# Cross attention on one Trainium2 core: the second token tile's queries are copied before the spread reciprocals instead of behind the first exponentials

## The reference, cut to what matters

```python
def _L0_xattn_ref(q, k, v, Wc, bc):          # q: layernorm of x; k = v = ctx_512
    b, s, _ = q.shape
    qh = q.reshape(b, s, N_GROUPS, HEADS_PER_GROUP, HEAD_DIM).transpose(0, 2, 3, 1, 4)
    kh = k.reshape(b, s, N_GROUPS, HEAD_DIM).transpose(0, 2, 1, 3)
    vh = v.reshape(b, s, N_GROUPS, HEAD_DIM).transpose(0, 2, 1, 3)
    scores = jnp.einsum('bghsd,bgtd->bghst', qh, kh) * scale
    probs = jax.nn.softmax(scores, axis=-1)
    out = jnp.einsum('bghst,bgtd->bghsd', probs, vh)
    out = out.transpose(0, 3, 1, 2, 4).reshape(b, s, D_MODEL)
    return out @ Wc.T + bc
x = x + _L0_attn_ref(_layernorm(x), ...)
x = x + _L0_xattn_ref(_layernorm(x), ctx_512, ctx_512, L0_xattn_Wc, L0_xattn_bc)
x = x + _L0_ffn_ref(_layernorm(x), ...)
```

## Time and profile before

| | |
|---|---|
| median of 3 runs | 2202.17 us |
| the profiled execution's own time | 2202.18 us |
| its span, first to last instruction | 2200.5 us |
| TensorE busy | 2022.2 us, 92% |
| VectorE busy | 1703.6 us, 77% |
| ScalarE busy | 1501.7 us, 68% |
| GpSimd busy | 702.2 us, 32% |
| mean granted TensorE clock | 0.962 |

### The profile page before, as it was taken

How to read it: one execution, slowest core, us unless ns; L and a number is a source line. 1 busy time by engine, 2 the same in 40 slices (tenths; PEclk the granted TensorE clock), 3 DMA queues, 4 the chain that set the end, 5 groups by cost and what they waited for, 6 DMA issues and landing times. The chain is left out here.

```text
span 2200.5 us, 54846 instructions
## 1 busy us (share of the span) xinstructions
PE 2022.2 (92%) x19284; PEld 1470.0 (67%) x19308; DVE 1703.6 (77%) x3951; ACT 1501.7 (68%) x4239; POOL 702.2 (32%) x601
## 2 busy tenths in 40 slices
PE   6799999999999999999999999769999999757998
PEld 3577777777777777777777777546666666434544
DVE  8778778787887877878878877546788888846997
ACT  2688878878878778878878878545665666633443
POOL 6311211211211121121121121204667777741332
PEclk9899999999999999999999999779999999978999
DMA  3000000000000000000000000063333332140111
GB/s 108 25 10 29 28 12 29 19 19 29 19 19 29 19 19 24 24 19 24 24 19 24 10 19 10 14 204 89 104 106 109 100 109 80 61 149 24 60 60 43
DMA packets 119444, 105.88 MB, mean 48 GB/s; under 512 B 11952, under 2 KB 93872, under 8 KB 119344
## 3 DMA queue, kind: packets, MB, share of 16 engines
q1 hardware_dynamic: 119344, 104.77, 15.2%
HBM read 70.66 MB, written 34.08 MB: 48 GB/s over the span
## 5 line engine op out<-in xcount | busy, mean ns | idle before, releaser
L714 PE MATMUL proj<-xn_hi,w_lo 128*128 x744 | 351.2, 472 | 0.0
L715 PE MATMUL proj<-xn_lo,w_hi 128*128 x744 | 294.6, 396 | 0.0
L716 PE MATMUL proj<-xn_hi,w_hi 128*128 x744 | 293.7, 395 | 0.0
L1101 DVE SCALAR_TENSOR_TENSOR qkv<-conv_in,taps,qkv 128x512 f32<-128x512 f32 x372 | 269.9, 746 | 0.0
L1328 POOL TENSOR_TENSOR o_scale<-o_var,neg_half 128x4 f32<-128x4 f32 x66 | 65.6, 1012 | 528.0 <-DVE o_var L1122 527.9
L1344 POOL TENSOR_TENSOR k_len<-sumsq,pos_half 128x4 f32<-128x4 f32 x31 | 45.5, 1467 | 554.3 <-DVE sumsq L1276 554.3
L1220 DVE TENSOR_TENSOR i_less_r<-bank_c,join_mask 128x256 f16<-128x256 f32 x320 | 120.7, 418 | 99.3 <-PE bank_c L777 98.8
L1020 ACT ACTIVATE inv<-bank_b 128x256 f16<-128x256 f32 x320 | 108.2, 382 | 91.5 <-PE bank_b L798 88.1
L716 PEld LDWEIGHTS proj<-xn_hi,w_hi 128*128 128x128 f32 x744 | 139.7, 188 | 33.4
L1825 ACT ACTIVATE probs_t<-ps_s 128x512 f32<-128x512 f32 x128 | 69.6, 596 | 133.8 <-PE ps_s L1673 133.7
L965 ACT ACTIVATE g_mask<-mask_ge,g_cols 128x128 fp32r<-128x128 f32 x512 | 153.3, 408 | 8.3 <-DVE g_cols L1304 8.3
(11 more groups left out here) (306 smaller groups left out, 5765.5 us busy)
## 6 DMA issues: line engine op xcount, KB each, us to landing
out_t<-o_out SPq DMA_DIRECT2D x66, 256.0 KB, 2.0
o_raw<-out_t SPq DMA_DIRECT2D x32, 512.0 KB, 5.3
w_raw<-in_L_attn_W_qkv_dram SPq DMA_DIRECT2D x32, 256.0 KB, 2.8
wq_dram<-wq_q SPq DMA_DIRECT2D x48, 128.0 KB, 1.8
x_sb<-in_x_dram SPq DMA_DIRECT2D x16, 256.0 KB, 2.7
w_raw<-in_L_attn_W_z_dram SPq DMA_DIRECT2D x16, 256.0 KB, 2.7
x_in<-in_x_dram SPq DMA_DIRECT2D x16, 256.0 KB, 6.0
wq_raw<-in_L_ffn_w_gate_dram SPq DMA_DIRECT2D x16, 256.0 KB, 2.8
```

The lines of the kernel that those rows point to most:

```text
L714: pe.matmul(out, w_lo[:, k, cols], sh.xn_hi[:, k, tok], start=(k == 0), stop=False)
L715: pe.matmul(out, w_hi[:, k, cols], sh.xn_lo[:, k, tok], start=False, stop=False)
L716: product = pe.matmul(out, w_hi[:, k, cols], sh.xn_hi[:, k, tok], start=False, stop=(k == KT - 1))
L1101: dve.scalar_tensor_tensor(out=out, in0=conv_in[:, j, :, k:k + T], scalar=taps[:, j, k:k + 1], in1=out, op0=ALU.mult, op1=ALU.add).then_in ...
```

## The change

ScalarE's call `queries(b, 1)` at (0,0) moves from behind `weigh(b, 0, 0)` to ahead of `spread(b - 1, 1)`. No instruction is added or taken away, no buffer or semaphore is changed, and the streams of the other engines are the same.

```diff
@@ -1848,10 +1848,9 @@
                             if (c, u) == (GROUPS - 1, 1):
                                 spread(b, 0)
                             if before and (c, u) == (0, 0):
+                                queries(b, 1)
                                 spread(b - 1, 1)
                             weigh(b, c, u)
-                            if before and (c, u) == (0, 0):
-                                queries(b, 1)
                             if before:
                                 if (c, u) == (0, 0):
                                     mixed(b - 1, 0)
```

## The result

The changed kernel takes 2184.01 us, the median of 4 runs (2182.72 to 2185.60); before it is 2202.31 us, the median of 4 (2200.81 to 2202.82). The ratio is 0.9918, with a 95% interval of 0.9901 to 0.9936. That is 18.3 us less, against 16.8 forecast; the forecast time was 2185.4 us, and the result lies inside its range. The profiled execution took 2185.60 us, its span is 2183.9 us.

The account below looks back on a forecast made before the run. TensorE was taken to set the pace, its idle time nearly all the keys' wait for the query copy. Gains of 5 x 2.61 + 1.37 + 2.35 = 16.8 us from 2202.2 gave 2185.4 us, range 2181 to 2194.

Parts of the forecast that it names:

- The new place costs nothing: ScalarE, after `probs_t`: the 0.62 us query copy fits the idle gap ahead of `r_chan`, 0.93 us at its smallest; cost 0.
- What becomes late next: TensorE, behind the keys: new waits of some 0.4 us at `turn_probs` and about 1 us at `mix`; step 2 gains 2.61 us.
- Steps as alike: Steps 1, 3, 4 and 6 taken as step 2: 5 x 2.61 us, plus 1.37 in step 5 and 2.35 in step 7.
- The clock: TensorE behind the two new gaps: no low clock, cost none; upper bound 1.24 us in each step, 8.7 us in all.
- I take the shift as kept in full: From `combine` on: TensorE had no wait in the step before, the other engines shift with it, so the whole gain stays.
- Rival C: Clock falls behind the gap ahead of `mix`, slowing `combine` by 3.0 us per step; slower, 2206.4 us; chance 0.03.
- Rival B: Nothing gained: TensorE waits as long at `mix`, or VectorE can't follow a shorter step; 2202 us; chance 0.05.

Follow-up runs that it names:

- experiment 4: Changed kernel with two more copies of the same queries, to unused tiles, ahead of the real copy in the new place; 2183.47 us, ratio to before 0.9923.
- experiment 1: Changed kernel with the query copy moved between the `r_chan` copy and the first exponentials; 2185.02 us, ratio to before 0.9923.
- experiment 5: Changed kernel with two of the four `k_blocks` copies of the keys' second half moved from ScalarE to VectorE; 2181.15 us, ratio to before 0.9903.
- Experiment 2: Kernel before, in its old order, with 22 TensorE transposes of the identity ahead of the keys; 2192.61 us, ratio to before 0.9958.
- experiment 6: Changed kernel with 22 TensorE transposes of the identity filling the wait ahead of `mix` in step 7 alone; 2182.94 us, ratio to before 0.9916.
- experiment 3: Changed kernel with the query copy one place earlier still, ahead of the last tile's `probs_t`; 2185.43 us, ratio to before 0.9930.
- experiment 7: Changed kernel with two `k_blocks` copies on VectorE, plus identity transposes filling TensorE's waits in step 7 and the drain; 2182.49 us, ratio to before 0.9911.

## Why the prediction was right

*The new place costs nothing.* Shown: the copy fills idle time, and experiment 4 used up this cover in step 7 and not before.

*What becomes late next.* The forecast named two waits, about 0.4 us at `turn_probs` and 1 us at `mix`; they are 0.46 and 0.97. It put `probs_t` 5.18 us and `combine` 6.67 us behind `r_chan`; they are at 5.18 and 6.67. The durations came from pairs of rows in which the same instructions follow one another without idling, and that is why they fit. Experiments 1 and 5 moved the chain from either side. One reading was loose: TensorE did have waits behind `combine` before, 0.37 us for `r_chan` once a step and the one for `r_sums` in step 6, but they hang on TensorE's own spreading and shifted with it.

*Steps as alike.* Taken at 2.61 us for five steps, 1.37 and 2.35 for the two others, the sum was 16.8. Measured at the start of `combine` the seven gains are 2.53, 2.61, 2.77, 2.77, 1.36, 2.52 and 2.59, together 17.15. Steps 3 and 4 gain more because the clock had fallen before the keys, which then were slow too. Step 7 was put too low, at 2.35, by a wrong term: the 2.73 us from `neg_max` to `mix` are TensorE's own pace in step 2, where its `mix` follows without idling. VectorE needs 2.42 from 1882.80, the start of `neg_max`, to the end of `mix_lo` in step 7 after.

*The clock.* The choice of no cost was right for steps 1 to 6: none of them has a spell behind the new waits, nor have the six such steps of the other kernels with this pattern; the one at the end of step 6 lies behind another wait and was there before. Experiment 2 gives the price of the old spells as 6.7 us in steps 1 to 6; the forecast's 1.24 us for five of them is 6.2, and the measured 6.7 are 1.34 each. The Trainium skill's rule on the price of a throttled spell ("TensorE: Matmul & The Clock Gate", section "Terms") would have made it, by the prediction's estimate, 1.5 us each, 7.5 in all; with the filling taken as the measure the rows' figure is nearer. The clock is low for 3.4 us in step 2, from 1608.7 to 1612.1, and not for the 3 us that this estimate took.

*The step that was wrong.* "I take the shift as kept in full", for step 7. Rival C, the clock falling on `combine` behind the wait at `mix`, was given 0.03 for all steps; it is what happened in step 7, where the forecast had computed a late `mix_lo` but not asked how long TensorE would then stand idle: 2.46 us, since step 7 has no projection piece. (With `probs_t` as the last to come, in experiments 1 and 4, the gap is 2.33 and 2.29 us and `combine` is as slow.) `combine` lost 1.54 us, and experiment 6 showed the gap to be the cause. The net gain up to the feed-forward part is 15.5 us and not 16.8. That the medians differ by more, 18.3, I can't assign: the parts of the program without a changed instruction vary by some 2 us between executions. That the measured time lies within 1.4 us of the forecast is in part luck, then; the gain per step is not.

*Rival B.* VectorE followed the shorter step; its waits for scores fell from 40.2 us to 16.0 in the same stretch of time, and none of the waits behind the changed place in steps 1 to 6 moved to it.

## What to carry to other kernels

When an in-order engine idles in front of one thing while another engine waits for something behind it, a copy whose input is long ready belongs in that idle gap; what it gains is read from the next wait down the chain, not from the wait that goes away. On TensorE price the wait together with the matmuls that run just after it, for nearly half of this gain was clock. And ask it of each step apart: here the last step, without its filler work, had a gap long enough to lower the clock where the others had none.

## What the runs showed of the hardware

The granted clock did not fall at a fixed distance from the end of a wait. In the kernel before it fell 0.4 us ahead of the restart in step 4, at it in steps 3 and 7, and 0.2 us behind it in step 2; in step 7 of the changed kernel it fell 1.2 us behind, so that `mix` and the first matmuls of `combine` ran at full speed and the rest at 1.2 GHz. Step 4 before, with the clock at 0.50 while TensorE is idle:

```profile
1724.80:1725.10 0.30, 0.00 (x0) 0.00 (x0) 0.00 (x0) 0.30 (x2) 0.30 (x2) 0.50 0.16 39
1725.16 1.12 PE L1651 MATMUL ps_c<-ident,k_rep 128*128 128x128 f32 x4 [2.59 <-ACT q_t L1797]
```

Single waits of 2.3 to 2.6 us lowered it in 11 of 12 cases (six of seven steps before, and step 7 of after and of experiments 1, 3, 4 and 5). Shorter ones did so in some executions and not in others: the wait of 1.97 us at the end of step 6 in five of nine (before, after, experiments 3, 4 and 6), that of 1.5 us in the drain in two of eight (after and experiment 6), that of 2.1 us behind it in two of six (before and experiment 2). Two gaps of 0.46 and 0.97 us with some 2.5 us of work between them did so in none of steps 1 to 6 of the changed kernel. Transposes of the identity into an unused bank, 22 in 2.6 us, kept it at 2.4 GHz where they filled waits of 2.59 and 2.46 us, and the work behind them started on time (experiments 2 and 6); ahead of a wait of 1.48 us the same 22 cost 0.8 us (experiment 7).
